# Second product and experts' last sum in two calls each, one column of ones in the key sums, and a new order of calls on all four compute engines

## What is computed

```
h = layernorm(x)
q, k, v = h @ Wq + bq, h @ Wk + bk, h @ Wv + bv          16 heads of 8 columns
qp, kp = elu(q) + 1, elu(k) + 1
kv = einsum('bshd,bshm->bhmd', kp, v);  ksum = sum(kp, axis=1)
z = 1 / (einsum('blhd,bhd->blh', qp, ksum) + 1e-6)
x = x + einsum('blhd,bhmd,blh->blhm', qp, kv, z) @ Wo + bo
x = x + relu(layernorm(x) @ W1 + b1) @ W2 + b2            W1: 128 to 512, W2: 512 to 128
```

## Time and profile before

| | |
|---|---|
| median of three runs | 589.15 us |
| the profiled execution's own time | 587.52 us |
| its span, first to last instruction | 585.7 us |
| PE busy | 563.1 us (96%) |
| PEld busy | 535.2 us (91%) |
| DVE busy | 429.4 us (73%) |
| ACT busy | 395.4 us (68%) |
| POOL busy | 258.6 us (44%) |
| granted TensorE clock | 1.00 in nearly the whole span (mean 1.000) |

### The profile page before, as it was taken

The page is one execution under the profiler, slowest core; times in us unless marked ns, Lnnn a source line. Parts: engine busy times, 40 slices in busy tenths (PEclk is TensorE's granted clock), DMA queues, the critical chain, the costliest instruction groups (busy, mean ns, idle before and its releaser), DMA issues.

```text
span 585.7 us, 13150 instructions
## 1 busy us (share of the span) xinstructions
PE 563.1 (96%) x4572; PEld 535.2 (91%) x4572; DVE 429.4 (73%) x1479; ACT 395.4 (68%) x1395; POOL 258.6 (44%) x431
## 2 busy tenths in 40 slices
PE   6899999999999999998999999999999999999997
PEld 3588999989999999998999999998999999999896
DVE  6967777678976777777886777767997666666785
ACT  3887688876666656787585566686686656666651
POOL 4443767464132465554412546545414334445420
PEclk9999999999999999999999999999999999999999
DMA  7700613100000000000000000000000000000000
GB/s 231 210 2 2 217 32 135 47 1 2 20 17 4 1 2 2 1 2 2 15 7 19 1 2 2 1 0 2 1 20 19 2 2 1 1 2 2 1 20 18
DMA packets 11049, 15.60 MB, mean 27 GB/s; under 512 B 960, under 2 KB 8224, under 8 KB 10600
## 3 DMA queue, kind: packets, MB, share of 16 engines
q1 hardware_dynamic: 8904, 12.54, 6.9%
q0 software_dynamic: 448, 1.25, 0.8%
q10 hardware_dynamic: 1632, 0.98, 0.6%
HBM read 12.63 MB, written 2.14 MB: 25 GB/s over the span
## 4 chain that ended last, share of the span: by engine, by line
PE 87%; ACT 6%; DVE 3%; issue 2%; POOL 1%; ACTq 1%; DVEq 0%; POOLq 0%
PE psB L1610 21%; PE psA L1610 20%; PE psD L1610 20%; PE psC L1610 18%; PE psC L1682 1%; PE psB L1682 1%; PE psD L1682 1%; PE psA L1682 1%; ACT L522 1%; ACT L476 1%; PE psD L1733 1%; PE psC L1733 1%; PE psB L1733 1%; PE psA L1733 1%; POOL xA L837 1%
## 5 line engine op out<-in xcount | busy, mean ns | idle before, releaser
L839 POOL TENSOR_TENSOR rstdD<-msD,neghalf 128x2 f32<-128x2 f32 x20 | 14.1, 704 | 54.1 <-ACT ziD L468 38.7
L839 POOL TENSOR_TENSOR rstdA<-msA,neghalf 128x2 f32<-128x2 f32 x20 | 14.1, 703 | 49.8 <-ACT eqkA L468 43.1
L1610 PE MATMUL psB<-w,H 128*128 128x128 f32 x256 | 31.7, 277 | 0.0
L1610 PE MATMUL psD<-w,H 128*128 128x128 f32 x256 | 31.3, 276 | 0.0
L1610 PE MATMUL psA<-w,H 128*128 128x128 f32 x256 | 31.2, 275 | 0.0
L1610 PE MATMUL psC<-w,H 128*128 128x128 f32 x256 | 31.2, 275 | 0.0
L1610 PEld LDWEIGHTS psC<-w,H 128*128 128x128 f32 x256 | 30.0, 192 | 0.0
L1610 PEld LDWEIGHTS psA<-w,H 128*128 128x128 f32 x256 | 30.0, 192 | 0.0
L1610 PEld LDWEIGHTS psD<-w,H 128*128 128x128 f32 x256 | 29.8, 191 | 0.0
L1610 PEld LDWEIGHTS psB<-w,H 128*128 128x128 f32 x256 | 29.8, 191 | 0.0
L839 POOL TENSOR_TENSOR rstdC<-msC,neghalf 128x2 f32<-128x2 f32 x20 | 13.9, 696 | 35.8 <-ACT eqkC L468 35.4
(11 more groups left out here) (584 smaller groups left out, 2357.6 us busy)
## 6 DMA issues: line engine op xcount, KB each, us to landing
M<-modulation_rows SPq DMA_DIRECT2D x2, 1280.0 KB, 9.5
M<-modulation_rows SPq DMA_DIRECT2D x1, 2560.0 KB, 8.6
out<-X SPq DMA_DIRECT2D x16, 128.0 KB, 1.9
M<-in_attn_W SPq DMA_DIRECT2D x3, 256.0 KB, 3.8
X<-in_attn_x_in ACTq DMA_DIRECT2D x2, 256.0 KB, 3.6
M<-in_attn_W ACTq DMA_DIRECT2D x1, 256.0 KB, 4.0
wo<-in_attn_Wo POOLq DMA_DIRECT2D x1, 256.0 KB, 4.4
wm<-in_wmod SPq DMA_DIRECT2D x1, 256.0 KB, 4.1
```

The source lines that it names most:

```text
L839: pool.tensor_tensor(b.rstd[:, :], b.ms[:, :], neghalf[:, :], ALU.pow).then_inc(b.s_rstd.sem, 1)
L1610: return pe.matmul(o, lhsT, rhs, start=start, stop=stop)
```

## The change

- `sums` makes 129 output columns in place of 144: the values and one column of ones. `masked` then needs two DVE instructions: the values times their mask, and the mask's 16 columns times the one sum, as a scalar of each partition. `attend` keeps its 144 columns.
- `contract` is called in two parts of four products, each after its own relu; only the second raises the counter. The parts add up in the same bank.
- `down` is called in two parts: the shared expert's and the first two blocks' six products, and the last two blocks' four.
- The lists of calls of PE, ACT, DVE and POOL are in a new order. PE's has 994 calls in place of 914 (the 80 second parts); ACT's 727, DVE's 849 and POOL's 357 calls are the same calls as before. SP's transfers are unchanged.

The diff, cut to the functions and to the places of the lists that the prediction speaks of:

```diff
             def masked(b, i, l):
 
                 dve.wait_ge(b.s_linps.sem, b.s_linps.value(i, 2 * l + 1))
-                dve.tensor_tensor(b.kv[:, :], b.ps[:, 1, 0:VW], headmask, ALU.mult).then_inc(b.s_kv.sem, 1)
+                dve.tensor_tensor(b.kv[:, 0:D], b.ps[:, 1, 0:D], headmask[:, 0:D], ALU.mult)
+                dve.tensor_scalar(b.kv[:, D:VW], headmask[:, D:VW], b.ps[:, 1, D:D + 1], None, ALU.mult)\
+                    .then_inc(b.s_kv.sem, 1)
...
                 for t in range(TILES):
-                    last = mm(b.ps[:, 1, 0:VW], b.kp[:, t, :], b.v[:, t, :], start=t == 0, stop=t == TILES - 1)
+                    last = mm(b.ps[:, 1, 0:D + 1], b.kp[:, t, :], b.v[:, t, 0:D + 1], start=t == 0, stop=t == TILES - 1)
                 last.then_inc(b.s_linps.sem, 1)
...
-            def contract(b, i, l):
-                pe.wait_ge(b.s_h.sem, b.s_h.value(i, (l + 1) * PAIRS))
-                if i == 0:
+            def contract(b, i, l, k):
+
+                pe.wait_ge(b.s_h.sem, b.s_h.value(i, l * PAIRS + k + 1))
+                if i == 0 and k == 0:
                     pe.wait_ge(s_w2, 2 * l + 2)
                 for t in range(TILES):
-                    for c in range(CH):
+                    for c in (2 * k, 2 * k + 1):
                         last = mm(b.ps[:, 0, t * P:(t + 1) * P], b.h[:, c, t * P:(t + 1) * P], w2[:, l, c, :],
-                                  start=c == 0, stop=c == CH - 1)
-                last.then_inc(b.s_w2ps.sem, 1)
+                                  start=c == 0 and t == 0, stop=c == CH - 1 and t == TILES - 1)
+                if k == PAIRS - 1:
+                    last.then_inc(b.s_w2ps.sem, 1)
...
-            def down(b, i):
-                order = (CH,) + tuple(range(CH))
-                pe.wait_ge(b.s_units.sem, b.s_units.of(EXPERT_UNITS, "product1", i))
-                for c in order:
-                    if c == 2:
-                        pe.wait_ge(b.s_units.sem, b.s_units.of(EXPERT_UNITS, "weighed1", i))
+            def down(b, i, part):
+
+                if part == 0:
+                    pe.wait_ge(b.s_units.sem, b.s_units.of(EXPERT_UNITS, "product1", i))
+                else:
+                    pe.wait_ge(b.s_units.sem, b.s_units.of(EXPERT_UNITS, "weighed1", i))
+                for c in ((CH, 0, 1), (2, 3))[part]:
...
```

ACT's list, end of the last layer:

```diff
                 transposed(C, i, 7)
                 squares(D_, i, 8)
+                relu(C, i, 3, 0)
+                tokensT(A, i)
                 transposed(D_, i, 7)
-                tokensT(A, i)
+                relu(D_, i, 3, 0)
                 tokensT(B, i)
-                relu(D_, i, 3, 0)
                 relu(D_, i, 3, 1)
                 router_exp(B, i)
-                relu(C, i, 3, 0)
                 router_exp(A, i)
```

PE's list, first layer's end (B and D before, then after) and the last layer with the experts of A and B:

```diff
-                contract(D_, i, 0)
+                expand(D_, i, 0, 1)
+                contract(D_, i, 0, 0)
                 out_project(B, i, 1)
+                contract(D_, i, 0, 1)
                 transposes(C, i, 2)
+                out_project2(B, i, 1)
+                if i == 0:
+                    fold_weights(7)
                 transposes(A, i, 3)
-                out_project2(B, i, 1)
-                if i == 0:
-                    fold_weights(7)
                 project_keys(C, i, 1)
                 project_queries(C, i, 1)
                 expand(A, i, 1, 0)
                 transposes(D_, i, 2)
...
                 attend(C, i, 3)
                 project_keys(D_, i, 3)
                 project_queries(D_, i, 3)
+                out_project(C, i, 3)
                 expand(B, i, 3, 0)
-                out_project(C, i, 3)
                 sums(D_, i, 3)
+                out_project2(C, i, 3)
                 expand(B, i, 3, 1)
-                out_project2(C, i, 3)
                 attend(D_, i, 3)
-                contract(B, i, 3)
+                contract(B, i, 3, 0)
+                contract(B, i, 3, 1)
                 out_project(D_, i, 3)
-                logits(A, i)
                 out_project2(D_, i, 3)
                 transposes(C, i, 7)
+                logits(A, i)
                 expand(C, i, 3, 0)
                 expand(C, i, 3, 1)
                 transposes(D_, i, 7)
+                logits2(A, i)
                 expand(D_, i, 3, 0)
-                logits2(A, i)
                 expand(D_, i, 3, 1)
                 logits(B, i)
                 gate(A, i, 2)
+                contract(D_, i, 3, 0)
+                logits2(B, i)
                 up(A, i, 2)
-                logits2(B, i)
```

PE's list, experts of C and D with the next step's first layer, after `logits2(D_, i)`:

```diff
                 logits2(D_, i)
-                gate(D_, i, 2)
                 logits2(C, i)
                 if i + 1 < STEPS:
                     project_keys(B, i + 1, 0)
-                up(D_, i, 2)
                 gate(C, i, 2)
-                gate(D_, i, 0)
+                up(C, i, 2)
                 if i + 1 < STEPS:
                     transposes(A, i + 1, 0)
                     project_queries(B, i + 1, 0)
-                up(C, i, 2)
+                gate(D_, i, 2)
+                up(D_, i, 2)
+                gate(D_, i, 0)
                 gate(C, i, 0)
                 up(D_, i, 0)
```

More of the change, by code:

```diff
@@ L594, in _ @@
                 att_transposed(A, i, 1)
+                squares(C, i, 3)
                 relu(D_, i, 0, 0)
@@ L1836, in down @@
                         hid = b.h[:, c, tok] if c < CH else b.hs[:, tok]
-                        last = mm(b.ps[:, 1, tok], hid, wd[:, c, :], start=c == order[0] and t == 0,
-                                  stop=c == order[-1] and t == TILES - 1)
-                last.then_inc(b.s_eps.sem, 1)
+                        last = mm(b.ps[:, 1, tok], hid, wd[:, c, :], start=c == CH and t == 0,
+                                  stop=c == CH - 1 and t == TILES - 1)
+                if part == 1:
+                    last.then_inc(b.s_eps.sem, 1)
             condition()
@@ L1905, in _ @@
                 project_queries(B, i, 1)
+                attend(A, i, 1)
                 transposes(D_, i, 1)
-                attend(A, i, 1)
-                contract(C, i, 0)
+                contract(C, i, 0, 0)
+                contract(C, i, 0, 1)
                 sums(B, i, 1)
@@ L1911, in _ @@
                 expand(D_, i, 0, 0)
-                expand(D_, i, 0, 1)
+                attend(B, i, 1)
                 if i == 0:
@@ L1923, in _ @@
                     fold_weights(7)
+                transposes(A, i, 3)
                 project_keys(C, i, 1)
@@ L1982, in _ @@
                 expand(B, i, 2, 1)
+                out_project2(C, i, 2)
                 attend(D_, i, 2)
-                out_project2(C, i, 2)
-                contract(B, i, 2)
+                contract(B, i, 2, 0)
+                contract(B, i, 2, 1)
                 out_project(D_, i, 2)
@@ L1995, in _ @@
                 sums(A, i, 3)
-                transposes(D_, i, 5)
                 project_keys(B, i, 3)
                 project_queries(B, i, 3)
+                contract(C, i, 2, 0)
                 attend(A, i, 3)
-                contract(C, i, 2)
+                transposes(D_, i, 5)
+                contract(C, i, 2, 1)
+                sums(B, i, 3)
                 out_project(A, i, 3)
                 expand(D_, i, 2, 0)
-                sums(B, i, 3)
                 expand(D_, i, 2, 1)
@@ L2015, in _ @@
                 project_queries(C, i, 3)
+                contract(A, i, 3, 0)
+                transposes(D_, i, 6)
                 sums(C, i, 3)
-                transposes(D_, i, 6)
-                contract(A, i, 3)
+                contract(A, i, 3, 1)
                 transposes(B, i, 7)
```

411 lines of the change are left out of this document (210 added, 201 removed).

## The result

The changed kernel takes 583.41 us (median of 5 runs, 582.88 to 583.91) against 589.15: a ratio of 0.9901, with a 95% interval of 0.9882 to 0.992. That is 5.7 us less, where 4.2 were forecast, and inside the range. As the experiments show, it is inside for partly wrong reasons: the order of the calls gave all of it, the shorter sums nothing on balance.

A forecast was written before the change was run, and what follows sets the result against it. PE, busy 96% of the span, was taken to set the time. Sums −2.6, order −1.6 and start 0 made −4.2 us against the median of 589.15, so 585.0 us, with a range of 577.0 to 589.7.

The forecast's parts named there:

- the signs named beforehand: Four sums within 0.45 us, layer 1's out_project2 showing 0.60, no wait before logits2(B), DVE +10 us, PE count 4572.
- Sums: PE's 256 sums instructions, 129 columns in place of 144, at 112 ns each: −2.6 us, bounds 0 and −2.9.
- Masked: DVE's masked in two instructions: about +0.15 us per call, bounds 0 and +0.30, hidden nearly everywhere.
- Splits: contract and down in two parts: no cost on PE, bounds −0.1 to +0.1 us per step.
- The order, per step: New lists of calls: −0.4 us per step, bounds −2.4 and +0.8; four times, −1.6 us.
- The list of waits: PE's waits per step before the change, read from the trace with 0.10 per first product: 4.8 us.
- The return of 0.4: New waits of 0.2 to 0.3 in two places, at transposes needing contract's later second half: +0.4 us per step.
- The exchange in the last layer: Waits of two expands (1.48) traded for about 1.3 at logits2(A): 0 per step, bounds −0.7 and +1.6.
- rival C: ACT's 1.6 us of inserted work ahead of transposed(D, i, 7) wholly exposed: +3.8, 593.0 us; chance 0.10.
- Experts of C and D: logits(D) and logits(C) earlier, gate(D, i, 2) later, losing its 0.3 wait: −0.3 us per step, bounds −0.7 and 0.
- `up(D, i, 0)`'s 0.4 stays: Second experts' stage: up(D, i, 0) keeps its 0.4 us wait, behind the router, which DVE takes after finish(A).
- The start: Calls ahead of the steps: one wait exchanged for another, with attend(B)'s 0.4; 0 us, bounds −0.8 and +1.0.

The follow-up runs named there:

- e2_order_only: The changed kernel with the edits of sums and masked undone (144 columns, one masked instruction), keeping new order and split calls: 583.29 us, ratio 0.9896.
- the best version: The changed kernel with masked's 16-column instruction as a product of two tensors in place of tensor by scalar: 580.92 us, ratio 0.986.
- the two halves run alone: Sums and masked edits alone on the kernel before: 590.68 us, ratio 1.0024; new order and split calls without those edits: 583.29 us, ratio 0.9896.
- e9_act_transposed_first: The best version with ACT's transposed(D, i, 7) moved ahead of relu(C, i, 3, 0) and tokensT(A): 588.51 us, ratio 0.9987.
- e8_contract_whole: The best version with contract(D, i, 0) and contract(B, i, 1) whole again, ahead of out_project: 583.39 us, ratio 0.9915.

## Why the prediction was right, and where it was not

**The total** held because two terms were wrong in opposite directions, which is luck. Forecast: sums −2.6, `masked` hidden, order −1.6. Measured: sums and `masked` together 0, order −5.9. Of the signs named beforehand, the spacing of the sums, the waits before `logits2(B)` and `out_project2(D, i, 1)` and PE's count came as said, and DVE's time nearly so; `out_project2(B, i, 1)` still shows 0.71, and the wait before `up(D, i, 0)` is gone.

**Sums.** The step was right and a little large: 112 ns each, as taken from the earlier trace rows, and 1.7 to 2.4 us for the whole where `masked` does not get in the way.

**Masked** is the step that failed. Its price, about +0.15 with bounds of 0 and +0.30, came from a 16-column operation that reads PSUM, and was held to be hidden. The new one reads its table in SBUF, the memory on the chip beside PSUM, and takes 0.23; together with the shorter first one the pair did cost some 0.14 more. But beside a POOL instruction on whole tensors it ended only just after that one, taking up to 1.65 us, and PE waited. In the changed order most of the loss is one such wait, in the first step. The row priced the work, not the wait for a resource that another engine held. The Trainium skill, "SBUF — State Buffer", section "Who interferes with whom", says just that: DVE and GpSimd share a pair of ports, which a tensor-by-scalar operation may take whole, and the second to come is blocked until the first has finished; a DVE instruction with one input in SBUF and no such mode is not concerned. The runs agree: 0.66 and 0.16 us for the same product in the two forms on the same order, beside the same calls of POOL. One thing does not fit: beside POOL's `rstd`, two columns in 0.70 us, the same instruction took its 0.23, so not every POOL instruction holds it up. The section of the Trainium skill that the prediction quoted for the overhead of small operations ("Perfetto Trace Analysis", "Optimizing Scalar/DVE Operations") names the shared port in its next paragraph; I had read it for the price alone.

**Splits.** Forecast 0 by themselves, and measured so (588.38 against 589.19, no difference that can be told).

**The order, per step** (second step, waits of PE before and after). The list of waits that it started from, 4.8 us, held two thirds of the 7.59.
- `out_project2(B, i, 1)` 0.30 to 0.21 and `(D, i, 1)` 0.30 to 0; forecast −0.6, got −0.4. The return of 0.4 came in size (0.24 here, 0.42 by the undone split), not in place: nothing waits at `transposes(D, i, 2)`, three calls of A and C do. Gross and net were thus 0.9 and 0.5 by experiment, 0.6 and 0.2 by forecast.
- `logits2(B)` 0.58 to 0.05, as forecast. `out_project2(D, i, 3)` 0.52 to 0.74, as forecast (its 0.52 had been read as 0.36 from the idle time). `out_project2(B, i, 2)` was to keep its 0.30; it went to 0.03, and `transposes(A, i, 5)` took 0.27. `out_project(C, i, 3)` with `expand(B, i, 3, 0)` +0.1, as forecast.
- The exchange in the last layer: two expands from 1.48 to 0.62, `logits2(A)` from 0.12 to 0.84, net −0.15 for a forecast of 0. But its price was argued the wrong way round. I counted ACT's new order as a cost that PE's order pays for; it is what makes PE's order possible, and with the old one 4.9 us are lost at this one call. Under PE's new order rival C had the sign wrong; ACT's new order under PE's old one was not run.
- `coef_transposes(B)` +0.11 for +0.3. The waits of `spread` that I had not listed changed chains (A 0.52 to 0, B 0.04 to 0.52).
- Experts of C and D: "`up(D, i, 0)`'s 0.4 stays" failed, it went (0.41 to 0.04). I held that the router waits for `finish(A)` on DVE; the list of DVE had changed too, and the earlier `logits` is worth 0.66 per step by experiment, 0.3 by forecast. This is the largest miss among the order's terms.

**The start**, forecast 0 within −0.8 and +1.0, fits where its order counts: from `transposes(A, 0, 0)` to the cut it is 0.25 us longer after, 0.13 in `e2_order_only`, and undoing it gained nothing. That is one execution of each, so its exact worth stays open. It was one wait for another: `attend(B, 0, 0)` waits 1.18 in place of 0.37, twice what was allowed for, and `out_project(A, 0, 0)` 0 in place of 0.41. The description of ACT's change was half right: `centre(D, 0)` stood ahead of `att_transposed(A, 0, 0)` before, too; new ahead of it are `squares(D, 0, 1)` and `high(1)`. The timed runs gained 1.9 us more than the two profiled ones (5.7 against 587.52 − 583.7 = 3.8); 1.3 of these lie in the stretch ahead of `transposes(A, 0, 0)`, the rest is open.

## What to carry to other kernels

Before a small operation is added to an engine with time to spare, look at what else its operands' memory serves at that moment: here the form of one 16-column product, more than its 0.07 us of length, decided over 2 to 4 us. In a kernel whose engines each follow a written list, a change of order on one engine has a price only together with the others' lists: one ACT call moved back cost 7.6 us of the 8.3 that the best version wins, some 4.9 by the wait and the rest by the clock that fell behind it. And a forecast that comes out right in total says little about its terms; only the two halves run alone showed that one of them was worth nothing on balance.

## What the runs showed of the hardware

That a DVE instruction's shown time includes its wait for POOL was not expected: 0.23 us became 0.66 and 1.65, each with its end just behind POOL's. It is no matter of tensor-by-scalar alone; a product of two tensors that both lie in SBUF, `scale(A)`, took 0.94 instead of 0.42, and in the changed kernel too it took 0.89 at 211.25, beside POOL's `add_bias`. Both ended 0.28 us after POOL's.

The start of the program differs between executions by PE's clock. In the changed kernel's execution the eight products from 8.88 took 1.91 us, where the ones before took 1.05, though the view shows 1.00 for both. In `e9_act_transposed_first` eight products of the same size at a granted 0.50 took just as long:

```profile
548.50 1.91 PE L1612 MATMUL psD<-w,H 128*128 128x128 f32 x8
```

So I take it that PE stood at the lower of its two levels (1.2 and 2.4 GHz) there as well.

The record also shows falls later in the start. In `e8_contract_whole`'s profile (stretch, length, PE's busy time and count, granted clock, share of DMA, GB/s) PE had been busy for 9.4 of 10 us at full clock, and then twice had 0.50 of it, for 3.4 us from 19.98 and for 6.8 us from 26.80, which gives these means:

```profile
10.00:20.00 10.00, 9.37 (x45) 1.00 0.94 272
20.00:30.00 10.00, 8.09 (x35) 0.67 0.53 149
30.00:40.00 10.00, 9.30 (x56) 0.82 0.01 2
```

There the 219th instruction came at 50.68 us; in the kernel before, with 1.00 in all of these stretches, at 46.27. What lowers it is open. It is why kernels were compared here by their steps as well as by their times.
